# A 3x3 convolution by minimal filtering F(4,3) instead of F(2,3) inside an attention-and-convolution kernel

## The reference, cut to what matters

```python
x = x + attention(gn(x))
y = gn(x)
y = relu(y * mask(y))                       # mask: abs, products, max(-1)
out = conv_general_dilated(y, weight, strides=(1, 1), padding=1)   # 256 -> 256 channels, 3 x 3
x = x + out + bias
```

## Time and profile before

| | |
|---|---|
| median of 3 timed runs | 350.37 us (348.88 to 351.1) |
| span of the profiled execution | 347.5 us |
| TensorE busy | 315.2 us, 91% |
| VectorE busy | 272.5 us, 78% |
| ScalarE busy | 148.8 us, 43% |
| GpSimd busy | 83.0 us, 24% |

### The profile page before, as it was taken

How to read it: one execution, slowest core, us unless ns; L and a number is a source line. 1 busy time by engine, 2 the same in 40 slices (tenths; PEclk the granted TensorE clock), 3 DMA queues, 4 the chain that set the end, 5 groups by cost and what they waited for, 6 DMA issues and landing times.

```text
span 347.5 us, 4162 instructions
## 1 busy us (share of the span) xinstructions
PE 315.2 (91%) x1566; PEld 222.3 (64%) x1566; DVE 272.5 (78%) x488; ACT 148.8 (43%) x189; POOL 83.0 (24%) x46
## 2 busy tenths in 40 slices
PE   0879968999979999999799999999799999999995
PEld 0566344267866663688567744888388727877884
DVE  4996668769999586889989767799887847897572
ACT  2442548464490843554047855351165423031300
POOL 2088513440436020003910200008600200202000
PEclk9999968899989999999999999999999999999999
DMA  8779500009700000099011200197001000101002
GB/s 276 276 102 140 228 5 0 2 1 134 94 0 4 2 1 2 0 130 159 1 63 41 82 1 2 35 128 128 4 0 62 0 0 5 58 0 62 0 0 121
DMA packets 12068, 20.38 MB, mean 59 GB/s; under 512 B 2065, under 2 KB 8081, under 8 KB 11793
## 3 DMA queue, kind: packets, MB, share of 16 engines
q1 hardware_dynamic: 12048, 20.13, 28.2%
HBM read 7.93 MB, written 4.19 MB: 35 GB/s over the span
## 4 chain that ended last, share of the span: by engine, by line
PE 58%; DVE 23%; ACT 8%; issue 6%; POOL 3%; DMA 2%; SPq 0%; DVEq 0%; POOLq 0%
PE slot L1113 29%; PE cps L1145 15%; PE slot L1189 7%; DVE l_max L848 3%; PE cps L1113 3%; DVE mask L784 3%; PE cps L1189 2%; ACT probs L563 2%; POOL probs L379 2%; DVE v_lo L814 1%; DMA xy<-x 1%; PE slot L1392 1%; ACT xn_hi L452 1%; ACT p_w L608 1%; DVE xn L740 1%
## 5 line engine op out<-in xcount | busy, mean ns | idle before, releaser
L1145 PE MATMUL cps<-v_hi,cw_hi 128*128 128x512 f32 (+1 forms) x144 | 57.6, 400 | 3.5 <-DVE v_lo L814 2.9
L1145 PE MATMUL cps<-v_hi,cw_lo 128*128 128x512 f32 (+1 forms) x144 | 57.9, 402 | 0.0
L1145 PE MATMUL cps<-v_lo,cw_hi 128*128 128x512 f32 (+1 forms) x144 | 56.4, 392 | 0.0
L379 POOL TENSOR_TENSOR probs<-q_w,k_w 128x1024 f32<-128x1024 f32 x14 | 32.9, 2376 | 79.5 <-DVE rw L777 72.3
L848 DVE TENSOR_REDUCE l_max<-slot 128x4 f32<-128x1024 f32 x32 | 37.1, 1216 | 5.9 <-PE slot L1113 5.9
L563 ACT ACTIVATE probs<-slot 128x1024 f32<-128x1024 f32 x32 | 31.4, 1021 | 16.0 <-PE slot L1113 15.9
L1145 PEld LDWEIGHTS cps<-v_hi,cw_hi 128*128 128x128 f32 x144 | 27.4, 191 | 12.7 <-issue 5.2
L1145 PEld LDWEIGHTS cps<-v_hi,cw_lo 128*128 128x128 f32 x144 | 27.4, 190 | 7.4 <-issue 2.2
L1145 PEld LDWEIGHTS cps<-v_lo,cw_hi 128*128 128x128 f32 x144 | 27.4, 190 | 5.0
L362 POOL TENSOR_TENSOR mask<-rw 128x1024 f32<-128x1024 f32 x8 | 15.2, 1912 | 56.6 <-DVE rw L777 56.6
L1113 PE MATMUL slot<-xn_hi,w_hi 128*128 128x512 f32 (+1 forms) x68 | 27.3, 401 | 1.1 <-ACT xn_hi L452 1.1
(11 more groups left out here) (197 smaller groups left out, 635.0 us busy)
## 6 DMA issues: line engine op xcount, KB each, us to landing
xy<-x SPq DMA_DIRECT2D x8, 512.0 KB, 6.6
out<-xy SPq DMA_DIRECT2D x8, 512.0 KB, 2.6
qs<-probs SPq DMA_DIRECT2D x12, 256.0 KB, 5.8
qs<-probs SPq DMA_DIRECT2D x24, 128.0 KB, 8.3
raw_cw<-conv_w SPq DMA_DIRECT2D x2, 1152.0 KB, 6.4
ks<-probs SPq DMA_DIRECT2D x12, 128.0 KB, 6.9
probs<-h_qkv SPq DMA_DIRECT2D x2, 192.0 KB, 3.8
probs<-l_kv SPq DMA_DIRECT2D x2, 128.0 KB, 3.7
```

What stands on the lines that cost most here:

```text
L379: nc.gpsimd.tensor_tensor(product(b, j).rearrange("p (n w) -> p n w", n=NW), q_w[:].rearrange("p (n w) -> p n w", n=NW), k_w[:, j * G:(j + ...
L1145: ins = nc.tensor.matmul(cps[:, pos % 2, y0 * WT:y1 * WT], (cw_hi, cw_hi, cw_lo)[part][:, k, pos, dy + 1, o * P:(o + 1) * P], (v_hi, v_lo, ...
```

## The change

F(4,3): four neighbouring output columns from six products instead of twelve. The input becomes six tiles of 256 columns in three groups of two (`NEAR`, `FAR`, `EDGE`), the weights six sets. An image takes 6 events x 36 matmuls of 256 columns (248 where a row is missing) = 216. One event is one of the six products for both output tiles, side by side in one bank. The two edge columns that the tiles need come from a padded buffer (`xn_rows`, 34 columns a row, zeroed by `pad`).

What moves with it: tiles are made for both input tiles at once; results are six events, which add a bank to one, two or three of the four column phases with a factor; the bias is now added by ScalarE (`add_bias`); the filling lists are 1.5 times as long in matmuls; the low part of EDGE is made in the next image's front; sums over channels, pooling, masks and tiles share other buffers (`mask` is gone, `v_hi` holds two groups, the tiles of the last image lie in `probs`), so the second load waits for image 0's products, and image 3's input is also loaded early into a free buffer for its moments; `store` waits for all of an image's events; the last image's results come in the order of its events.

```diff
-POS = 4
-WT = W // 2
+GROUPS = 3
+TW = W // 4
+N4 = H * TW
-EVENTS = KT * POS
+ORDER = ((NEAR, 0), (FAR, 0), (NEAR, 1), (FAR, 1), (EDGE, 0), (EDGE, 1))
+EVENTS = len(ORDER)
+EVENT_MM = 2 * POS_MM
+CONV_MM = EVENTS * EVENT_MM
-EARLY = 8
-REST = (4, 3, 5, 3, 4, 8)
-FRONT = (0, 11, 0, 0, 4, 3, 3, 3, 3, 3, 6, 10, 18)
-POOL_WAIT = 8
+EARLY = 12
+REST = (6, 5, 8, 5, 6, 12)
+FRONT = (0, 17, 0, 0, 6, 4, 4, 4, 4, 4, 9, 15)
+POOL_WAIT = 12
...
+            weights = Chain(pool, cw_pool, CW_POOL, 0)
+            def low_weights():
+                link, t, far = weights, taps[1], cw_new[:, 1, FAR]
+                for k in (1, 0):
+                    pool.wait_ge(cw_act, 6 - k)
+                    for i in range(2):
+                        link(weight_low(nc.gpsimd, k, NEAR, i))
+                pool.wait_ge(soft_c, N_SOFT)
+                link(nc.gpsimd.tensor_scalar(far[:, 1], t[:, 2], 4.0, 0.0, ALU.mult, ALU.add))
+                link(nc.gpsimd.tensor_tensor(far[:, 1], far[:, 1], t[:, 0], ALU.add))
+                link(nc.gpsimd.tensor_scalar(t[:, 1], t[:, 1], 2.0, 0.0, ALU.mult, ALU.add))
+                link(nc.gpsimd.tensor_tensor(far[:, 0], far[:, 1], t[:, 1], ALU.add))
+                link(nc.gpsimd.tensor_tensor(far[:, 1], far[:, 1], t[:, 1], ALU.subtract))
...
                 if b == 1:
-                    mask_sum(0, 2)
-                    pool.wait_ge(v_dve, KT)
+                    mask_sum(0)
+                    pool.wait_ge(v_dve, 1)
                     pool.wait_ge(lv_pe, 1)
                 products(b)
...
+            def add_bias(b, o):
+                act.wait_ge(yn_ready, b * KT + o + 1)
+                nc.scalar.activation(img(b, o), img(b, o), ACT.Identity, bias=cbias[:, o:o + 1]).then_inc(biased, 1)
...
+                if g == NEAR:
+                    nc.vector.scalar_tensor_tensor(to[:, 0], columns(1), -4.0, columns(3), ALU.mult, ALU.add)
+                    tile_step(nc.vector.scalar_tensor_tensor(to[:, 1], columns(2), -4.0, columns(4), ALU.mult, ALU.add))
+                    tile_step(nc.vector.tensor_tensor(to[:, 1], to[:, 1], to[:, 0], ALU.subtract))
+                    last = nc.vector.scalar_tensor_tensor(to[:, 0], to[:, 0], 2.0, to[:, 1], ALU.mult, ALU.add)
+                elif g == FAR:
+                    tile_step(nc.vector.tensor_tensor(to, columns(3, 2), columns(1, 2), ALU.subtract))
+                    tile_step(nc.vector.scalar_tensor_tensor(to[:, 1], to[:, 0], -2.0, to[:, 1], ALU.mult, ALU.add))
+                    last = nc.vector.scalar_tensor_tensor(to[:, 0], to[:, 0], 4.0, to[:, 1], ALU.mult, ALU.add)
...
+            def far_weights(link):
+                t, to = taps[0], cw_new[:, 0, FAR]
+                link(nc.vector.scalar_tensor_tensor(to[:, 1], t[:, 2], 4.0, t[:, 0], ALU.mult, ALU.add))
+                link(nc.vector.scalar_tensor_tensor(to[:, 0], t[:, 1], 2.0, to[:, 1], ALU.mult, ALU.add))
+                link(nc.vector.scalar_tensor_tensor(to[:, 1], t[:, 1], -2.0, to[:, 1], ALU.mult, ALU.add))
+                dve.wait_ge(cw_act, 4)
+                for k in range(KT):
+                    link(edge_low(nc.vector, k, 0))
...
+            def conv_result(b, e):
...
+                if e == 0:
+                    ins = into(odd, 2.0, twice(m))
+                elif e == 1:
+                    into(y[:, 1], 0.5, m)
+                    ins = into(y[:, 3], 2.0, m)
+                elif e == 2:
+                    into(y[:, 2], 1.0, m)
+                    ins = into(odd, -1.0, twice(m))
+                elif e == 3:
+                    into(y[:, 0], 0.125, m)
+                    into(y[:, 1], -0.25, m)
+                    ins = into(y[:, 2], 0.5, m)
+                elif e == 4:
+                    ins = into(y[:, 0], 1.0, m)
+                else:
+                    ins = into(y[:, 3], -1.0, m)
...
             def front(b, older=None, first=False):
...
                     query_lo(b)
                     key_lo(b)
                     dve.wait_ge(y_ready, b * KT)
+                    older_result(2)
+                    conv_low(older, EDGE)
                     row_sums(b - 1)
                     column_sums(b - 1)
                     normalisation(b - 1, 1)
                     mask_parts(b - 1)
                 maxima(b, range(6))
-                older_result(V_SUM)
+                older_result(3)
                 maxima(b, range(6, NB))
                 maxima_parts(b)
-                older_result(V_DIFF)
                 if not first:
                     for k in range(KT):
                         masked_image(b - 1, k)
-                    conv_tiles(b - 1, 0, 0)
+                    pad(b - 1)
+                    conv_tiles(b - 1, NEAR)
                 window_maxima(b)()
                 if first:
-                    turned_taps(weights)
+                    far_weights(weights)
+                older_result(4)
                 if not first:
-                    conv_tiles(b - 1, 1, 0)
...
+                    conv_low(b - 1, NEAR)
+                    conv_tiles(b - 1, FAR)
+                older_result(5)
...
+                    conv_tiles(b - 1, EDGE)
+                    conv_low(b - 1, FAR)
...
+                    if g == NEAR:
+                        step_out(nc.vector.tensor_tensor(y, y, m[:, 0].unsqueeze(1).to_broadcast([P, 4, N4]), ALU.add))
+                        into(even, 1.0, twice(m[:, 1]))
+                        ins = into(odd, -1.0, twice(m[:, 1]))
+                    elif g == FAR:
+                        for j in range(4):
+                            ins = into(y[:, j], 0.125 * 2 ** j, m[:, 0])
+                        step_out(ins)
+                        for j in range(4):
+                            ins = into(y[:, j], 0.125 * (-2) ** j, m[:, 1])
+                    else:
+                        into(y[:, 0], 1.0, m[:, 0])
+                        ins = into(y[:, 3], -1.0, m[:, 1])
```

More of the change, by code:

```diff
@@ L492, in normalise, with edge_weights, weight_high @@
                     nc.scalar.copy(xn_hi[:, k], xn[:, k]).then_inc(xhi_ready, 1)
[L494 to L496 removed]
+            def edge_weights(k):
+                for i in range(2):
+                    nc.scalar.copy(cw_hi[:, k, EDGE, i], taps[k][:, 2 * i]).then_inc(cw_act, 1)
+            def weight_high(k, g):
+                nc.scalar.copy(cw_hi[:, k, g].rearrange("p s r c -> p (s r c)"),
+                               cw_new[:, k, g].rearrange("p s r c -> p (s r c)")).then_inc(cw_act, 1)
             def values_of(s):
@@ L1054, in last_front @@
+                last_low(0, NEAR)
+                last_tiles(0, FAR)
                 column_sums(b, slice(1, 2), mask_last[1])
-                conv_tiles(b, 0, 1)
-                conv_result(older, (POS + V_LEFT, POS + V_RIGHT))
-                conv_low(b, 0, 1)
+                last_low(0, FAR)
+                last_tiles(0, EDGE)
+                conv_result(older, 5)
                 mask_parts(b, slice(1, 2), mask_last[1])
+                last_low(0, EDGE)
                 masked_image(b, 1)
-                for phase in range(2):
-                    conv_tiles(b, 1, phase)
-                    conv_low(b, 1, phase)
+                pad(b, range(1, 2))
@@ L1150, in more, with conv_mm @@
+                        hi, lo = tile_hi(b, g)[:, side, k], v_lo[:, g, side, k]
+                        ins = conv_mm(cps[:, e % 2, o * N4:(o + 1) * N4], g, side, o, k, m, hi, lo,
+                                      e < 2 and o == k == m == 0)
+                        if (i + 1) % EVENT_MM == 0:
                             ins.then_inc(conv_pe, 1)
                     self.at += n
+            def conv_mm(to, g, side, o, k, m, hi, lo, first):
+                row, part = divmod(m, 3)
+                dy = ROW_ORDER[k][row]
+                y0, y1 = max(0, -dy), min(H, H - dy)
+                return nc.tensor.matmul(to[:, y0 * TW:y1 * TW],
+                                        (cw_hi, cw_hi, cw_lo)[part][:, k, g, side, dy + 1, o * P:(o + 1) * P],
+                                        (hi, lo, hi)[part][:, (y0 + dy) * TW:(y1 + dy) * TW],
+                                        start=first, stop=k == KT - 1 and m == POS_MM // KT - 1,
+                                        skip_group_check=True)
```

515 lines of the change are left out of this document (274 added, 241 removed).

## The result

| | before | after |
|---|---|---|
| time, median | 350.09 us | 413.18 us (4 executions, 412.61 to 413.58) |
| profiled execution: span | 347.5 us | 411.5 us |
| mean granted clock of TensorE | 0.979 | 0.864 |

The changed kernel is slower by a ratio of 1.181 (95% interval 1.177 to 1.186). The forecast was 365.4 us and the range ended at 376: the sign was right, but the loss forecast (15 us) was a quarter of the real one (63 us).

The account below looks back on a forecast made before the run. TensorE and VectorE were both taken as nearly full, each bounding some stretches, with VectorE leading mid-period. Terms 5 + 4.5 + 0 + 0 + 4.5 + 1 = +15 on 350.4 gave 365.4 us, range 347 to 376.

Parts of the forecast that it names:

- the sign: Whole kernel: the change makes it slower, chance 0.80 (faster 0.13, same 0.07).
- the price of the stride: VectorE's tiles and results: elements four apart cost nothing extra, with 0 to 2 us a period kept as bound.
- the other terms: Start +5, image 1 +4.5, images 2 and 3 0, end +4.5 and last stores +1: together +15 us.
- Rival C: TensorE, idle more, gets half clock more often: four more stretches on the path at 1.7 us each, 372 us; chance 0.09.
- TensorE: Convolution matmuls start every 0.120 us, 25.9 us an image instead of 32.8, taking 27.6 us off TensorE in all.
- rival D: Weight loads bound each TensorE pair at 0.188 us: 40.6 us an image, 382 us in all; chance 0.02.
- Rival A: TensorE remains the bound (91% busy) and its gain comes through: 340 us at full effect, faster; chance 0.15.
- Start: 0 to 59 us: VectorE's five tap operations collide with GpSimd's, delaying the first product; +5 us, bounds 0 to 6.
- Image 1: 59 to 130 us: FAR tiles pass between GpSimd's products, 2.6 us of work taking 7 to 9; +4.5, bounds 1 to 7.
- Images 2 and 3: 130 to 278 us: maxima end 3.2 us later, 3.4 gained afterwards; called 0 per period, bounds -5 and +3.
- End: 278 to 347.5 us: VectorE's tiles and results end the kernel, +4.5 (bounds -1 and +7), and last stores +1 (0 to 2).
- VectorE's busy time: Whole kernel: VectorE busy some 288 us instead of 272.5.

Follow-up runs that it names:

- e3: Changed kernel with VectorE's convolution results and input tiles both on neighbouring elements instead of every fourth (sums land in wrong columns): 376.84 us, ratio 1.077.
- e1: Changed kernel with only VectorE's convolution results on neighbouring elements instead of every fourth one: 395.38 us, ratio 1.130.
- e16: Kernel before without a third of its convolution matmuls (192, 43.8 us of TensorE): 341.38 us, ratio 0.975.
- e17: e3 without the same third of its convolution matmuls (288, 34.6 us of TensorE): 381.41 us, ratio 1.096.
- e10: e3 with VectorE's convolution results treating 32 elements of each run instead of 256 or 512: 365.25 us, ratio 1.037.
- e11: Kernel before with VectorE's convolution results on 32 elements instead of 512: 348.00 us, ratio 0.986.
- e6: e3 with GpSimd's five FAR tap operations after image 0's first product, ScalarE's FAR weight copies behind image 1's normalisation: 375.62 us, ratio 1.070.
- e7: e3 with GpSimd's products of image 1 waiting for the low part of image 0's FAR tiles instead of NEAR: 376.12 us, ratio 1.074.
- e8: e3 with VectorE's FAR tiles of image 0 behind all row maxima instead of between them: 374.90 us, ratio 1.072.
- e15: Changed kernel with paired result elements and rectified image stored by column phase, plus the repairs of e6 and e8: 397.00 us, ratio 1.132.
- e9: e3 with extra TensorE work in image 0's softmax and product stage (16 constant matmuls, second window values computed ten times): 388.42 us, ratio 1.104.

## Why the prediction was wrong

**The step that failed** is the price of the stride: "A stride of four elements in image and result isn't in the trace; a stride of two costs nothing, so I take nothing and keep 0 to 2 us a period." It costs 0.41 us on 512 elements and 0.82 on 1024; for the results of one of the first three images 8 x 0.41 + 2 x 0.82 = 4.9 us, for the tiles 6 x 0.42 + 0.83 = 3.4: 8.3 us a period, where the bound was 2. With nothing else changed, e3 shows it to be 36 us of the 63. The nearest rows reached to a stride of two only; a bound that says "as for two" wasn't one. Without the stride the kernel still takes 376.84 us, so the sign wasn't luck, but the other terms, at +15, were too small as well: they came to 27.

**Rival C** named something that did happen, at a size far too small: not four more stretches at half clock but 97 us more. To see what of it lies on the path I added up TensorE's pieces of the chain that lie in windows at half clock: 12 us before, 60 after, 31 in e3. Half of each is what the lower clock costs: 6, 30 and 16 us. So of the 64 us of span some 24 are the clock's, and 14 of the 36 that e3 won back. This is an accounting on one profile each, not an experiment. It isn't a cause apart, since the clock moved with the stride in e1 to e3; the likely reading is that VectorE's longer operations make TensorE wait, and the wait costs again as clock.

**TensorE**: 0.120 us a matmul was right (0.116), and so rival D was wrong. That this takes work off TensorE was right at full clock and of no use (e16, e17). Rival A, for which I took TensorE's 91% as the argument, is refuted by e10 beside e11, and by e17.

**Start**: first product forecast at 57 to 60, seen at 59.94; the five operations alternate with GpSimd's (0.95, 1.46, 2.47, 2 x 1.97) and e6 shows 4.0 us at this place. The Trainium skill, "SBUF — State Buffer", section "Who interferes with whom", has such instructions exclude each other, and the trace agrees. Missed: 2.9 us before that, from projections that ran at half clock from 20 to 27 us, which before they had not (granted clock from 20 to 30 us: 1.00 before, 0.66 after, the third digit of the clock row above), and 2.3 us in the product stage at half clock. +5 was +8.8, outside 0 to 6.

**Image 1**: the FAR tiles stretched as forecast (7.6 us for three operations). But little or nothing came back when it was removed (0.7 us in e7, 1.9 in e8, none in e15): in e7 the window scores behind GpSimd's products were waited for next. +4.5 was +10.3 without the stride; beyond the collision the cause is open, but the clock (0.87 against 0.95) may have a part in it.

**Images 2 and 3**: 0 with bounds of -5 and +3; e3 shows +3.8 and +3.2, just outside. For image 3 the terms can be read in e3: the maxima end 2.7 us later after the per-head group (forecast 3.2), VectorE's list from there to the first product takes 20.9 us (20.2), and from the first product to the next per-head group it takes 11.7 us where it was 9.8: 1.2 shorter was forecast, and it is 1.9 longer. So there the product stage is the term that failed. In image 2 it is the maxima, 4.3 us later.

**End**: predicted +5.5; e3 +1.6, after +14.8. In the changed kernel VectorE works through and TensorE is done 10 us earlier (forecast: 4 or more), with every result at the wide price (beside the earlier trace rows):

```profile
389.62 2.02 DVE L1230 TENSOR_TENSOR xy<-xy,slot 128x1024 f32<-128x1024 f32 x1
...
395.74 12.48 DVE L1007 SCALAR_TENSOR_TENSOR xy<-slot,xy 128x512 f32<-128x512 f32 x22
```

**VectorE's busy time** was to be 288 us. Even e3 has 299.9: of the 12 us more, 4.0 are the taps at the start and 6.3 the FAR tiles and their low part beside GpSimd, times that were counted as waits on the path but not as busy.

## What to carry to other kernels

Before a transform is exchanged for one with fewer multiplications, price its additions by their addresses: operations of VectorE and ScalarE whose fp32 elements lie 16 bytes apart took 1.4 to 1.8 times as long here (256 to 1024 elements), while two elements used out of each 16 bytes cost VectorE nothing, so that the order of the loops inside one instruction can decide. Before work is taken off an engine that is 91% busy, take a part of it away for a trial: 44 us of its matmuls were worth 8 here. Where two engines share the chain, an added microsecond on one can cost more than itself (31.4 us were worth 36.3), with the other waiting more and granted its lower clock longer. And when work is moved out of a collision, look at what runs in the new place: e6 won 4.0 us at the old one and made another chain 5.6 us longer.

## What was not expected of the hardware

- An operation on VectorE of 480 elements takes 0.68 us at a stride of one or two elements, 0.82 at three and 1.02 at four; input or output alone is enough for it.
- ScalarE took 1.125 us for 512 elements that it reads four apart, 0.63 for 512 neighbours and 1.067 for 1024.
- VectorE's operations on 2 elements per partition, 0.16 us each, took up to 1.68 us beside GpSimd's of 1.8 us (e6).
- TensorE was halved for 20 us in a stretch in which it was busy for 18.8 of them, after one pause of 1.08 us (e9).
